# Fused GroupNorm attention block: normalisation of an image moved twelve slots ahead, and a new order of the first images' products

## The chip, the cores and the metric

One core of one Trainium2 chip runs the whole program in one launch. The metric is the device time of an execution in microseconds. The kernel before takes 1676.67 us (median of 3 runs, 1676.18 to 1676.68).

## The reference, cut to what matters

x has 16 images of 192 channels and 32 x 32 = 1024 positions, float32. Only a normalisation without weights, one attention block and the residual are computed:

```python
def _gn(v, G=32, eps=1e-05):
    g = v.reshape(B_, G, C_ // G, H_, W_)
    m = jnp.mean(g, axis=(2, 3, 4), keepdims=True)
    s = jnp.var(g, axis=(2, 3, 4), keepdims=True)
    return ((g - m) / jnp.sqrt(s + eps)).reshape(v.shape)
def attention(x, qkv_w, proj_w, proj_b):      # 6 heads of 32 channels, N = 1024
    xt = x.reshape(B, C, N).transpose(0, 2, 1)
    qkv = jnp.einsum('bnc,oc->bno', xt, qkv_w)
    q, k, v = ...
    attn = jax.nn.softmax(jnp.einsum('bhnd,bhmd->bhnm', q, k) * SCALE, axis=-1)
    out = jnp.einsum('bhnm,bhmd->bhnd', attn, v).transpose(0, 2, 1, 3).reshape(B, N, C)
    return (jnp.einsum('bnc,oc->bno', out, proj_w) + proj_b).transpose(0, 2, 1).reshape(B, C, H, W)
return x + attention(_gn(x), qkv_w, proj_w, proj_b)
```

## The kernel before, in words

**Steps and slots.** The program is a list of 20 steps, at = -3 to 16, and step b >= 0 attends to image b. A step has 24 slots: 3 pairs of heads, each with 8 tiles of 128 keys. A slot has 4 score units (two heads, two halves of 512 queries); "(5, 3)" is unit 3 of slot 5. Each engine has its own loop over steps, slots and units, and runs its instructions strictly in that order; nothing reorders them, and semaphores alone tie the engines together. Which slot a piece of work stands in is written out by hand in the tables at lines 57 to 80.

**What one slot does while a step attends.** TensorE makes 4 score products into 2 banks (line 535), ScalarE takes the exponential of each (line 690), TensorE weighs the values of the slot before (line 550, after unit 1), GpSimd adds the exponentials of two slots in pairs (line 743, in odd slots) and twice more in slots 3, 11 and 19 (line 749), and TensorE counts these sums (line 567). Beside that it makes 4 products for the row maxima of tiles 12 slots ahead, into 3 banks (line 469), and VectorE reduces each (line 844). From slot 12 of a step on these maxima are those of the next image, so in step -1 slots 12 to 23 make the maxima that image 0 needs before its first score. Scores of 2 banks mean that TensorE is at most two scores ahead of ScalarE, and maxima of 3 banks that it is at most three ahead of VectorE.

**Extras.** One PSUM bank, extra_ps, serves all other TensorE work, one extra in a slot (fill, line 473, in units 2 and 3), and the next extra waits until the one before is read (extra_freed). An extra is a "shift" (the transposed row maxima), a "v" product (read by ScalarE, line 613), a "qk" product (rounded by ScalarE, line 610, its remainder by VectorE, line 880), or a "proj" product (line 873). VectorE and ScalarE read an extra at the start of the slot after it. In step b, slots 3, 4 and 6 make qk products of image b+1, slots 7, 8, 11 and 14 its v, and slots 12, 16 and 19 the first qk products of image b+2. SyncE then stacks q and k with 18 DMAs in three sixes (slots 7, 9, 11, line 350). Step -2 makes all six qk products of image 0 (QK_FIRST_SLOTS) and stacks them, step -1 the v of image 0 and the first three qk products of image 1.

**The normalisation of image b+3 before.** x is loaded in slot 10 of step b (line 436, 3 DMAs), its statistics are taken by VectorE in slots 16 and 17 (line 776, 4 instructions), SyncE takes them to DRAM in slot 18 and back by groups in slot 20 (lines 370 and 375), VectorE aggregates in (22, 2) (line 786 to 790) and GpSimd makes the factors in slot 23 (lines 758 and 761). In step b+1 SyncE takes the factors to DRAM in slot 0 and back by channels in slot 1 (lines 358, 363, 365), ScalarE writes the normalised image in 8 instructions in slots 3 to 9 (line 642), and GpSimd the remainders in slots 8 and 10 (lines 708 and 718).

**SyncE.** It issues every DMA of the kernel in program order and waits in place for what a DMA needs. Around the change stand: the row shifts of a pair in slots 6, 14 and 22 (line 394, waited for by the first score of slots 8, 16 and 0), the sums spread in slots 5, 13 and 21 (line 400, waited for by VectorE's reciprocal at the end of slots 6, 14 and 22), their way back in slots 7/8, 15/16 and 23/0 (lines 407 and 413), the attention output's moves in slots 6, 14 and 23 (line 427), the residual's load in slot 4 (line 432) and the store of the image before in slot 23 (line 439).

Of the kernel before, what the change touches and what calls it, by code (L numbers as in the profile page):

```python
# [10 lines left out]
ALU = mybir.AluOpType  # L11
# [4 lines left out]
BATCH = 16  # L16
C = 192
# [4 lines left out]
GROUPS = 32  # L22
GROUP = C // GROUPS
# [4 lines left out]
P = 128  # L28
# [5 lines left out]
CB = C - P  # L34
# [22 lines left out]
SHIFT_SLOTS = {5: 1, 13: 2, 21: 0}  # L57


STATS_AT = ((16, 1), (16, 3), (17, 1), (17, 3))  # L60
STATS_OUT_SLOT, STATS_IN_SLOT = 18, 20
AGGREGATE_AT = (22, 2)
RSTD_SLOT = 23
NORM_OUT_SLOT, NORM_IN_SLOT = 0, 1
XHAT_AT = ((3, 3), (4, 1), (5, 3), (6, 1), (6, 3), (7, 3), (9, 1), (9, 3))
XLO_SLOTS = (8, 10)

QK_FIRST_SLOTS = (12, 13, 14, 15, 16, 17)
QK_SECOND_SLOTS = (17, 19, 22)
V_SECOND_SLOTS = (14, 15, 18, 20)  # L70
V_SLOTS = (7, 8, 11, 14)
QK_SLOTS = (12, 16, 19)
QK_LATE_SLOTS = (3, 4, 6)
# [3 lines left out]
assert len(set(EXTRA_SLOTS)) == len(EXTRA_SLOTS)  # L77
STACK_SLOTS = {7: 0, 9: 1, 11: 2}
QK_READERS = ((0, 1), (0, 2), (1, 2))
LOAD_SLOT = 10  # L80

PAIR = 2
PAIR_COUNTED = PAIR + 3
# [22 lines left out]
XHAT = 8  # L106
# [6 lines left out]
class Step:  # L113
# [5 lines left out]
    def __init__(self, b, at, extras):  # L119
        self.b = b  # L120
        self.parity = at % 2
        self.attend = 0 <= at < BATCH
        self.follow = 0 <= at + 1 < BATCH
        self.project_in = 0 <= at + 2 < BATCH
        self.take_stats = 0 <= at + 3 < BATCH
        self.tail = 0 <= at - 1 < BATCH
        self.qk_slots = {-2: QK_FIRST_SLOTS, -1: QK_SECOND_SLOTS}.get(at, QK_SLOTS)
        self.v_slots = V_SECOND_SLOTS if at == -1 else V_SLOTS
        self.late = at >= 0 and self.follow
        self.extras = extras  # L130

    def extra(self, s):

        if s in SHIFT_SLOTS and (self.follow if SHIFT_SLOTS[s] == 0 else self.attend):
            return "shift", SHIFT_SLOTS[s]
        if self.follow and s in self.v_slots:
            return "v", self.v_slots.index(s)
        if self.project_in and s in self.qk_slots:
            return "qk", self.qk_slots.index(s)
        if self.late and s in QK_LATE_SLOTS:  # L140
# [55 lines left out]
def group_norm_attention(nc, x, qkv_wT, proj_wT, proj_b, identity, out):  # L196


    with ExitStack() as ctx:
# [125 lines left out]
        def _(sp):  # L325
# [27 lines left out]
            def step(st):  # L353
                b = st.b
                for s in range(SLOTS):
                    if st.project_in and s == NORM_OUT_SLOT:
                        sp.wait_ge(rstd_step, 2 * (b + 3))
                        sp.dma_start(norm_rows[:, :].rearrange("(g c) k -> g c k", c=GROUP),
                                     group_norm[:, :].unsqueeze(1).broadcast_to([GROUPS, GROUP, 2])
                                     ).then_inc(norm_out, MOVE)  # L360
                    if st.project_in and s == NORM_IN_SLOT:
                        sp.wait_ge(norm_out, MOVE * (b + 3))
                        sp.dma_start(chan_norm[:, 0, :], norm_rows[0:P, :]).then_inc(norm_in, MOVE)
                        for r in range(2):
                            sp.dma_start(chan_norm[CB * r:CB * (r + 1), 1, :],
                                         norm_rows[P:C, :]).then_inc(norm_in, MOVE)
# [6 lines left out]
                    if st.take_stats and s == STATS_IN_SLOT:  # L373
                        sp.wait_ge(stats_out, 2 * MOVE * (b + 4))
                        sp.dma_start(group_stats[:, :],
                                     stats_rows[:, :].rearrange("(g c) k -> g (c k)", c=GROUP)
                                     ).then_inc(stats_in, MOVE)
                    if s == QK_FIRST_SLOTS[-1] + 1 and not st.follow and st.project_in:
# [50 lines left out]
                    if s == 4 and st.tail:  # L429
# [4 lines left out]
                    if s == LOAD_SLOT and st.project_in and b + 3 < BATCH:  # L434
                        sp.wait_ge(xhat_ready, XHAT * (b + 3))
                        load_x(b + 3)
# [160 lines left out]
        def _(act):  # L597
# [34 lines left out]
            def normalise(st, k):  # L632

                t, hi, half = k // 4, k // 2 % 2, k % 2
                if k == 0:
                    act.wait_ge(norm_in, 3 * MOVE * (st.b + 3))
                    if due(st.b + 2):

                        act.wait_ge(xlo_ready, LO * (st.b + 2))
                n = slice(HALF * half, HALF * (half + 1))  # L640
                to = (xhat[:, t, n], (xhat_a_hi, xhat_b)[t][:, st.parity, n])[hi]
                nc.scalar.activation(to, x_sb[:, t, n], ACT.Identity, bias=chan_norm[:, t, 1:2],  # L642
                                     scale=chan_norm[:, t, 0:1]).then_inc(xhat_ready, 1)

# [56 lines left out]
        def _(pool):  # L701
            nc.gpsimd.memset(k_stack[STACK:SHIFTED, :, :, :], SHIFT).then_inc(shift_set, 1)

            def step(st):
                for s in range(SLOTS):
                    if st.project_in and s == XLO_SLOTS[0]:
                        pool.wait_ge(xhat_ready, XHAT * (st.b + 2) + XHAT // 2)
                        nc.gpsimd.tensor_tensor(xhat_a_lo[:, st.parity, :], xhat[:, 0, :],  # L708
                                                xhat_a_hi[:, st.parity, :], ALU.subtract).then_inc(xlo_ready, 1)
                    if st.project_in and s == XLO_SLOTS[1]:  # L710
                        pool.wait_ge(xhat_ready, XHAT * (st.b + 3))

                        if st.attend:
                            was, q = divmod(s // PAIR - 1, PAIRS_A_HEAD)
                            pool.wait_ge(pairs_added, READY[-1] * (PAIRS * st.b + was) + READY[q])
                        else:
                            pool.wait_ge(xlo_ready, 2 * (st.b + 2) + 1)
                        nc.gpsimd.tensor_tensor(xhat_b[CB:P, st.parity, :], xhat[CB:P, 1, :],  # L718
                                                xhat_b[CB:P, st.parity, :], ALU.subtract).then_inc(xlo_ready, 1)
                        pool.wait_ge(xlo_ready, 2 * (st.b + 3))  # L720
                    for j, par, p in st.due(s, DIVIDED, TILES):

                        k = PAIRS * j + p
# [216 lines left out]
```

## Time and profile before

| what | number |
| --- | --- |
| median of 3 runs | 1676.67 us |
| the profiled execution | 1676.28 us |
| its span | 1674.5 us |
| mean granted TensorE clock | 0.982 |
| TensorE busy | 1556.8 us (93%) |
| VectorE, ScalarE, GpSimd busy | 1188.9, 1232.9, 1321.8 us |
| chain that ended last | TensorE 80%, ScalarE 10% |

The span runs from the first to the last instruction. Busy shares are averages over a start of some 112 us without scores, 16 steps of some 96 us, and an end of some 45 us. A matmul's end is modelled, so TensorE's busy time also covers short waits; its real waits are read from the starts of its instructions and from the waits of its weight loads.

### The profile page before, as it was taken

What the parts mean: (1) busy time and instruction counts of PE and PEld (TensorE: products, weight loads), DVE (VectorE), ACT (ScalarE), POOL (GpSimd) and SP (SyncE); (2) the same over time, 40 slices, a digit from 0 to 9 for tenths busy, and PEclk for the clock granted to TensorE, in tenths of its full rate; (3) what the DMA queues carried; (4) which work ended last, traced back from release to release, by engine and by line L of the source; (5) the groups of instructions that cost most, each with busy time, mean ns of one, the idle gap of its engine ahead of it and who ended that gap; (6) DMA issues with size and microseconds to landing.
All of it is one profiled execution on the core that took longest, in us unless ns stands there. A gap on an engine that the chain in (4) does not pass through costs nothing.

```text
span 1674.5 us, 24581 instructions
## 1 busy us (share of the span) xinstructions
PE 1556.8 (93%) x8800; PEld 488.0 (29%) x8800; DVE 1188.9 (71%) x2022; ACT 1232.9 (74%) x2001; POOL 1321.8 (79%) x645
## 2 busy tenths in 40 slices
PE   3389999999999999999999999999999999999982
PEld 1123233232323333232332323232332323233220
DVE  3387878777787877777787777778787777777710
ACT  2138787887869787886968788796978778686770
POOL 3019888888978888888888888897888888788891
PEclk9979999999999999999999999999999999999995
DMA  2304042341515134152504325151513414141112
GB/s 71 57 26 83 15 88 47 75 86 52 103 38 103 27 85 76 52 108 52 95 25 94 57 68 93 52 103 38 98 34 77 83 52 83 52 71 33 46 34 68
DMA packets 86106, 108.87 MB, mean 65 GB/s; under 512 B 38240, under 2 KB 50912, under 8 KB 85984
## 3 DMA queue, kind: packets, MB, share of 16 engines
q1 hardware_dynamic: 85984, 107.30, 30.8%
q8 instruction: 70, 1.15, 0.3%
q14 instruction: 52, 0.43, 0.1%
HBM read 42.98 MB, written 13.15 MB: 34 GB/s over the span
## 4 chain that ended last, share of the span: by engine, by line
PE 80%; ACT 10%; issue 2%; DMA 1%; DVE 1%; SPq 0%; POOL 0%; POOLq 0%; ACTq 0%; DVEq 0%
PE heads_ps L550 21%; PE scores_ps L535 19%; PE max_ps L469 19%; PE sums_ps L567 7%; ACT probs L690 6%; PE extra_ps L518 2%; PE extra_ps L522 2%; PE extra_ps L519 2%; PE extra_ps L520 2%; PE extra_ps L523 2%; ACT heads_sb L653 1%; ACT xhat_b L642 1%; ACT x_res L620 1%; DMA inv_sb<-inv_rows 1%; PE extra_ps L498 0%
## 5 line engine op out<-in xcount | busy, mean ns | idle before, releaser
L844 DVE TENSOR_REDUCE half_max<-max_ps 128x1 f32<-128x512 f32 x1536 | 1005.2, 685 | 336.0 <-PE max_ps L469 321.8
L690 ACT ACTIVATE probs<-scores_ps,exp_scale 128x512 f32<-128x512 f32 x1536 | 994.1, 689 | 310.4 <-PE scores_ps L535 304.5
L743 POOL TENSOR_TENSOR prob_pairs<-probs 128x1024 f32<-128x1024 f32 x384 | 898.6, 2361 | 205.1 <-ACT probs L690 204.2
L469 PE MATMUL max_ps<-k_stack,q_stack 96*128 96x512 f16 x1536 | 593.5, 388 | 22.5 <-DVE half_max L844 13.5
L535 PE MATMUL scores_ps<-q_stack,k_stack 98*128 98x512 f16 x1536 | 586.4, 383 | 24.4 <-ACT probs L690 18.2
L550 PE MATMUL heads_ps<-probs,v_sb 128*32 128x512 f32 x3072 | 409.8, 606 | 0.1
L469 PEld LDWEIGHTS max_ps<-k_stack,q_stack 96*128 96x128 f16 x1536 | 149.7, 98 | 555.5 <-issue 429.6
L749 POOL TENSOR_TENSOR prob_pairs<-prob_pairs 128x1024 f32<-128x1024 f32 x96 | 224.3, 2358 | 0.0
L535 PEld LDWEIGHTS scores_ps<-q_stack,k_stack 98*128 98x128 f16 x1536 | 149.5, 98 | 237.3 <-ACT probs L690 171.3
L567 PE MATMUL sums_ps<-prob_pairs,ones 128*32 128x512 f32 x1152 | 154.3, 608 | 3.2 <-POOL prob_pairs L743 3.2
L550 PEld LDWEIGHTS heads_ps<-probs,v_sb 128*32 128x32 f32 x3072 | 60.5, 108 | 131.7 <-issue 129.9
L880 DVE TENSOR_TENSOR qk_lo<-extra_ps,qk_hi 128x512 f16<-128x512 f32 x96 | 65.8, 686 | 33.4 <-ACT qk_hi L610 33.4
L727 POOL TENSOR_TENSOR heads_out<-heads_sb,inv_sb 128x512 f32<-128x512 f32 x48 | 61.0, 1271 | 32.8 <-DMA inv_sb<-inv_rows 26.8
L642 ACT ACTIVATE xhat<-x_sb,chan_norm 128x512 f32<-128x512 f32 x64 | 51.2, 806 | 46.3 <-DMA chan_norm<-norm_rows 46.3
L610 ACT CAST qk_hi<-extra_ps 128x512 f16<-128x512 f32 x96 | 56.0, 583 | 35.5 <-PE extra_ps L523 35.5
L873 DVE SCALAR_TENSOR_TENSOR x_res<-extra_ps,proj_unscale,x_res 96x512 f32<-96x512 f32 x64 | 46.1, 720 | 50.2 <-PE extra_ps L523 50.2
L758 POOL TENSOR_TENSOR group_norm<-var_eps,minus_half 32x1 f32<-32x1 f32 x16 | 8.6, 540 | 67.9 <-issue 64.2
L732 POOL TENSOR_TENSOR heads_lo<-heads_out,heads_hi 128x512 f16<-128x512 f32 x48 | 55.6, 1159 | 1.5 <-ACT heads_hi L630 1.5
L518 PE MATMUL extra_ps<-xhat_a_hi,w_hi 128*128 128x512 f16 x96 | 38.0, 396 | 17.9 <-POOL xhat_b L718 10.1
L708 POOL TENSOR_TENSOR xhat_a_lo<-xhat,xhat_a_hi 128x1024 f16<-128x1024 f32 x16 | 34.6, 2165 | 19.2 <-ACT xhat_a_hi L642 19.2
L776 DVE BATCH_NORM_STATS2 half_stats<-x_sb 128x6 f32<-128x512 f32 x64 | 43.3, 684 | 8.0 <-DMA x_sb<-x 8.0
L518 PE MATMUL extra_ps<-attn_a_hi,wp_hi 128*96 128x512 f16 x64 | 25.4, 397 | 22.9 <-DMA attn_b<-heads_lo 20.3
(82 smaller groups left out, 940.0 us busy)
## 6 DMA issues: line engine op xcount, KB each, us to landing
q_stack<-qk_hi SPq DMA_DIRECT2D x96, 128.0 KB, 4.2
k_stack<-qk_hi SPq DMA_DIRECT2D x96, 128.0 KB, 5.6
inv_sb<-inv_rows SPq DMA_DIRECT2D x48, 256.0 KB
x_res<-x SPq DMA_DIRECT2D x16, 768.0 KB, 5.5
out<-x_res SPq DMA_DIRECT2D x16, 768.0 KB, 4.6
x_sb<-x SPq DMA_DIRECT2D x16, 512.0 KB, 7.4
x_sb<-x SPq DMA_DIRECT2D x32, 256.0 KB, 8.7
q_stack<-qk_lo SPq DMA_DIRECT2D x48, 128.0 KB, 4.1
```

The costliest lines, as they stand in the source:

```text
L469: pe.matmul(max_ps[:, bank, :], q_stack[0:STACK, par, h, P * tile:P * (tile + 1)], k_stack[0:STACK, par, h, HALF * half:HALF * (half + 1)] ...
L518: pe.matmul(to, hi[:, 0, :], a_hi, start=True, stop=False)
L535: pe.matmul(scores_ps[:, u_bank(s, u), :], k_stack[0:SHIFTED, st.parity, h, P * tile:P * (tile + 1)], q_stack[0:SHIFTED, st.parity, h, HAL ...
L550: last = pe.matmul(heads_ps[at:at + D, :], v_sb[:, par, tile, D * h:D * (h + 1)], probs[:, a, s % RING, HALF * half:HALF * (half + 1)], st ...
L567: last = pe.matmul(sums_ps[at:at + D, :], ones[:, 0:D], prob_pairs[:, a, at_pair, HALF * half:HALF * (half + 1)], start=(at_pair == QUAD_A ...
L642: nc.scalar.activation(to, x_sb[:, t, n], ACT.Identity, bias=chan_norm[:, t, 1:2], scale=chan_norm[:, t, 0:1]).then_inc(xhat_ready, 1)
L690: nc.scalar.activation(probs[:, a, s % RING, HALF * half:HALF * (half + 1)], scores_ps[:, u_bank(s, u), :], ACT.Exp, scale=exp_scale[:, 0: ...
L727: nc.gpsimd.tensor_tensor(heads_out[:, :], heads_sb[:, (par + p) % 2, :], inv_sb[:, :], ALU.mult).then_inc(divided, 1)
L743: nc.gpsimd.tensor_tensor(prob_pairs[:, a, q, :], probs[:, a, (s - 1) % RING, :], probs[:, a, s % RING, :], ALU.add).then_inc(pairs_added, 1)
L749: nc.gpsimd.tensor_tensor(prob_pairs[:, a, q, :], prob_pairs[:, a, q, :], prob_pairs[:, a, q - 1, :], ALU.add).then_inc(pairs_added, 1)
L844: nc.vector.tensor_reduce(half_max[:, a, tile, half:half + 1], max_ps[:, bank, :], AX_X, ALU.max).then_inc(max_read[bank], 1)
L880: nc.vector.tensor_tensor(qk_lo[:, t, n], extra_ps[:, :], qk_hi[:, t, n], ALU.subtract).then_inc(extra_freed, 1)
```

## The change

The tables put the same work in other slots, and the blocks of SyncE, ScalarE and GpSimd are tied to the step that takes the statistics. The whole normalisation of image b+3 is now within step b: load in slot 0, statistics in slots 5 and 6, to DRAM in 7 and back in 9, aggregate in (10, 2), factors in 11, factors to DRAM in 12 and back in 13, the normalised image in unit 1 of slots 15 to 22, remainders in 19 and 23. In step -2 the six qk products of image 0 are in slots 0 to 5 and the 18 stacking DMAs in slot 6, ahead of the statistics' way out in slot 7. In step -1 the first qk products of image 1 are in slots 0, 2 and 4 and v of image 0 in slots 7, 8, 11 and 14. No instruction is added or removed.

```diff
-STATS_AT = ((16, 1), (16, 3), (17, 1), (17, 3))
-STATS_OUT_SLOT, STATS_IN_SLOT = 18, 20
-AGGREGATE_AT = (22, 2)
-RSTD_SLOT = 23
-NORM_OUT_SLOT, NORM_IN_SLOT = 0, 1
-XHAT_AT = ((3, 3), (4, 1), (5, 3), (6, 1), (6, 3), (7, 3), (9, 1), (9, 3))
-XLO_SLOTS = (8, 10)
-
-QK_FIRST_SLOTS = (12, 13, 14, 15, 16, 17)
-QK_SECOND_SLOTS = (17, 19, 22)
-V_SECOND_SLOTS = (14, 15, 18, 20)
+STATS_AT = ((5, 1), (5, 3), (6, 1), (6, 3))
+STATS_OUT_SLOT, STATS_IN_SLOT = 7, 9
+AGGREGATE_AT = (10, 2)
+RSTD_SLOT = 11
+NORM_OUT_SLOT, NORM_IN_SLOT = 12, 13
+XHAT_AT = ((15, 1), (16, 1), (17, 1), (18, 1), (19, 1), (20, 1), (21, 1), (22, 1))
+XLO_SLOTS = (19, 23)
+
+QK_FIRST_SLOTS = (0, 1, 2, 3, 4, 5)
+QK_SECOND_SLOTS = (0, 2, 4)
-LOAD_SLOT = 10
+LOAD_SLOT = 0
...
-        if self.follow and s in self.v_slots:
-            return "v", self.v_slots.index(s)
+        if self.follow and s in V_SLOTS:
+            return "v", V_SLOTS.index(s)
...
+                    if s == LOAD_SLOT and st.project_in and b + 3 < BATCH:
+                        sp.wait_ge(xhat_ready, XHAT * (b + 3))
+                        load_x(b + 3)
...
-                    if st.project_in and s == NORM_OUT_SLOT:
-                        sp.wait_ge(rstd_step, 2 * (b + 3))
+                    if st.take_stats and s == NORM_OUT_SLOT:
+                        sp.wait_ge(rstd_step, 2 * (b + 4))
...
-                    act.wait_ge(norm_in, 3 * MOVE * (st.b + 3))
-                    if due(st.b + 2):
+                    act.wait_ge(norm_in, 3 * MOVE * (st.b + 4))
+                    if due(st.b + 3):
...
-                to = (xhat[:, t, n], (xhat_a_hi, xhat_b)[t][:, st.parity, n])[hi]
+                to = (xhat[:, t, n], (xhat_a_hi, xhat_b)[t][:, 1 - st.parity, n])[hi]
...
-                if st.project_in and (s, u) in XHAT_AT:
+                if st.take_stats and (s, u) in XHAT_AT:
...
-                    if st.project_in and s == XLO_SLOTS[0]:
-                        pool.wait_ge(xhat_ready, XHAT * (st.b + 2) + XHAT // 2)
+                    if st.take_stats and s == XLO_SLOTS[0]:
+                        pool.wait_ge(xhat_ready, XHAT * (st.b + 3) + XHAT // 2)
```

## Rows read from the trace of the kernel before

**Rows 1.** Busy time by engine in step 6: us, PE, PEld, DVE, ACT, POOL, clock, DMA.

```profile
684.80:780.70 95.90, 94.73 (x551) 30.04 (x549) 73.64 (x126) 76.85 (x125) 81.88 (x41) 1.00 0.32 70
```

**Rows 2.** Timeline of the start: start us, us, instruction, [idle before, releaser].

```profile
10.22 0.85 SPq L370 DMA_DIRECT2D stats_rows<-half_stats  x2
...
14.02 0.47 DVE L786 BATCH_NORM_AGGREGATE group_mv<-group_stats 32x2 f32<-32x72 f32 x1 [1.23 <-DMA group_stats<-stats_rows]
...
22.26 1.52 ACT L642 ACTIVATE xhat<-x_sb,chan_norm 128x512 f32<-128x512 f32 x2 [20.24 <-DMA chan_norm<-norm_rows]
...
30.53 0.58 PE L518 MATMUL extra_ps<-xhat_a_hi,w_hi 128*128 128x512 f16 x1 [10.12 <-POOL xhat_b L718]
...
48.97 1.28 DVE L776 BATCH_NORM_STATS2 half_stats<-x_sb 128x6 f32<-128x512 f32 x2
...
52.80 0.64 SPq L350 DMA_DIRECT2D q_stack<-qk_hi  x1
...
64.41 0.58 SPq L375 DMA_DIRECT2D group_stats<-stats_rows  x1
69.92 0.47 DVE L786 BATCH_NORM_AGGREGATE group_mv<-group_stats 32x2 f32<-32x72 f32 x1 [17.15 <-DMA group_stats<-stats_rows]
...
71.59 0.61 SPq L358 DMA_DIRECT2D norm_rows<-group_norm  x1
...
78.08 1.52 ACT L642 ACTIVATE xhat<-x_sb,chan_norm 128x512 f32<-128x512 f32 x2 [26.04 <-DMA chan_norm<-norm_rows]
...
86.49 0.48 ACT L613 COPY v_sb<-extra_ps 128x384 f32<-128x384 f32 x1 [2.30 <-PE extra_ps L502]
...
112.58 0.63 PE L535 MATMUL scores_ps<-q_stack,k_stack 98*128 98x512 f16 x1
```

**Rows 3.** Timeline of VectorE in slots 5 to 7 of step 6.

```profile
706.09 2.47 DVE L844 TENSOR_REDUCE half_max<-max_ps 128x1 f32<-128x512 f32 x4
...
708.78 0.28 DVE L861 SCALAR_TENSOR_TENSOR shift_rows<-extra_ps,shift_rows 16x128 f16<-16x128 f32 x1
...
712.90 0.69 DVE L880 TENSOR_TENSOR qk_lo<-extra_ps,qk_hi 128x512 f16<-128x512 f32 x1 [0.40 <-ACT qk_hi L610]
```

**Rows 4.** Timeline of TensorE in slots 6 and 7 of step 6, the first matmul of each extra.

```profile
709.72 0.38 PE L518 MATMUL extra_ps<-xhat_a_hi,w_hi 128*128 128x512 f16 x1
...
713.74 0.25 PE L498 MATMUL extra_ps<-w_hi,xhat_a_hi 128*128 128x192 f16 x1
```

**Rows 5.** Waits, slots 4 to 10 of step 6: total us, times, longest.

```profile
PEld scores_ps L535 <- ACT probs L690: 2.8, 7, 0.9
```

**Rows 6.** Waits, slots 15 to 22 of step 6.

```profile
ACT probs L690 <- PE scores_ps L535: 9.6, 16, 1.4
...
PEld scores_ps L535 <- ACT probs L690: 1.5, 5, 0.5
```

**Rows 7.** Timeline of GpSimd in step 6: slot 0, slots 10 and 12.

```profile
686.82 0.54 POOL L758 TENSOR_TENSOR group_norm<-var_eps,minus_half 32x1 f32<-32x1 f32 x1
...
726.92 2.13 POOL L718 TENSOR_TENSOR xhat_b<-xhat,xhat_b 64x1024 f16<-64x1024 f32 x1
...
735.01 4.67 POOL L749 TENSOR_TENSOR prob_pairs<-prob_pairs 128x1024 f32<-128x1024 f32 x2
```

**Rows 8.** Timeline of SyncE in step 6: slots 0 and 14.

```profile
687.64 0.62 SPq L358 DMA_DIRECT2D norm_rows<-group_norm  x1
...
741.16 1.22 SPq L394 DMA_DIRECT2D q_stack<-shift_rows  x2
```

**Rows 9.** The 16 stores of the factors (line 358), from issue to landing.

```profile
DMA to landing us min/median/max: 3.3/4.1/5.6
```

**Rows 10.** Timeline of VectorE and ScalarE, end of slot 14 to slot 16 of step 6.

```profile
744.09 0.24 DVE L899 RECIPROCAL inv_spread<-sums_spread 128x16 f32<-128x16 f32 x1
...
745.67 1.27 ACT L690 ACTIVATE probs<-scores_ps,exp_scale 128x512 f32<-128x512 f32 x2 [0.60 <-PE scores_ps L535]
747.73 1.27 ACT L690 ACTIVATE probs<-scores_ps,exp_scale 128x512 f32<-128x512 f32 x2 [0.79 <-PE scores_ps L535]
```

More of the change, by code:

```diff
@@ L127, in __init__ @@
         self.qk_slots = {-2: QK_FIRST_SLOTS, -1: QK_SECOND_SLOTS}.get(at, QK_SLOTS)
-        self.v_slots = V_SECOND_SLOTS if at == -1 else V_SLOTS
         self.late = at >= 0 and self.follow
@@ L355, in step @@
                 for s in range(SLOTS):
-                    if st.project_in and s == NORM_OUT_SLOT:
-                        sp.wait_ge(rstd_step, 2 * (b + 3))
[L358 to L366, printed above, removed]
+                    if s == LOAD_SLOT and st.project_in and b + 3 < BATCH:
+                        sp.wait_ge(xhat_ready, XHAT * (b + 3))
+                        load_x(b + 3)
                     if st.take_stats and s == STATS_OUT_SLOT:
@@ L377, in step @@
                                      ).then_inc(stats_in, MOVE)
+                    if st.take_stats and s == NORM_OUT_SLOT:
+                        sp.wait_ge(rstd_step, 2 * (b + 4))
+                        sp.dma_start(norm_rows[:, :].rearrange("(g c) k -> g c k", c=GROUP),
+                                     group_norm[:, :].unsqueeze(1).broadcast_to([GROUPS, GROUP, 2])
+                                     ).then_inc(norm_out, MOVE)
+                    if st.take_stats and s == NORM_IN_SLOT:
+                        sp.wait_ge(norm_out, MOVE * (b + 4))
+                        sp.dma_start(chan_norm[:, 0, :], norm_rows[0:P, :]).then_inc(norm_in, MOVE)
+                        for r in range(2):
+                            sp.dma_start(chan_norm[CB * r:CB * (r + 1), 1, :],
+                                         norm_rows[P:C, :]).then_inc(norm_in, MOVE)
                     if s == QK_FIRST_SLOTS[-1] + 1 and not st.follow and st.project_in:
@@ L433, in step @@
                                      x[b - 1, :, :].rearrange("(t p) n -> p t n", p=OM)).then_inc(res_loaded, MOVE)
-                    if s == LOAD_SLOT and st.project_in and b + 3 < BATCH:
-                        sp.wait_ge(xhat_ready, XHAT * (b + 3))
-                        load_x(b + 3)
                     if s == SLOTS - 1 and st.tail:
@@ L635, in normalise @@
                 if k == 0:
-                    act.wait_ge(norm_in, 3 * MOVE * (st.b + 3))
-                    if due(st.b + 2):
-                        act.wait_ge(xlo_ready, LO * (st.b + 2))
+                    act.wait_ge(norm_in, 3 * MOVE * (st.b + 4))
+                    if due(st.b + 3):
+                        act.wait_ge(xlo_ready, LO * (st.b + 3))
                 n = slice(HALF * half, HALF * (half + 1))
-                to = (xhat[:, t, n], (xhat_a_hi, xhat_b)[t][:, st.parity, n])[hi]
+                to = (xhat[:, t, n], (xhat_a_hi, xhat_b)[t][:, 1 - st.parity, n])[hi]
                 nc.scalar.activation(to, x_sb[:, t, n], ACT.Identity, bias=chan_norm[:, t, 1:2],
@@ L705, in step @@
                 for s in range(SLOTS):
-                    if st.project_in and s == XLO_SLOTS[0]:
-                        pool.wait_ge(xhat_ready, XHAT * (st.b + 2) + XHAT // 2)
[L708 to L711, printed above, removed]
+                    if st.take_stats and s == XLO_SLOTS[0]:
+                        pool.wait_ge(xhat_ready, XHAT * (st.b + 3) + XHAT // 2)
+                        nc.gpsimd.tensor_tensor(xhat_a_lo[:, 1 - st.parity, :], xhat[:, 0, :],
+                                                xhat_a_hi[:, 1 - st.parity, :], ALU.subtract).then_inc(xlo_ready, 1)
+                    if st.take_stats and s == XLO_SLOTS[1]:
+                        pool.wait_ge(xhat_ready, XHAT * (st.b + 4))
                         if st.attend:
@@ L716, in step @@
                         else:
[L717 to L720, printed above, removed]
+                            pool.wait_ge(xlo_ready, 2 * (st.b + 3) + 1)
+                        nc.gpsimd.tensor_tensor(xhat_b[CB:P, 1 - st.parity, :], xhat[CB:P, 1, :],
+                                                xhat_b[CB:P, 1 - st.parity, :], ALU.subtract).then_inc(xlo_ready, 1)
+                        pool.wait_ge(xlo_ready, 2 * (st.b + 4))
                     for j, par, p in st.due(s, DIVIDED, TILES):
```

## The prediction

> **What bounds the kernel now.** I read the busy time of one steady step first, then the timeline of the start, then, slot by slot, the timelines around the old and the new places of the moved work. A steady step lasts 95.9 us and TensorE is busy in 94.7 of them [rows 1]; the other engines have 14 to 22 us to spare. So a moved piece costs something only where it makes TensorE wait, and helps only where TensorE waits for it now. The direct sign of such waits is the weight load of a score that waits for an exponential: 2.8 us in slots 4 to 10 of a step [rows 5] and 1.5 us in slots 15 to 22 [rows 6]. It starts earlier than the matmul's own wait, so it is an upper bound. Ahead of the steady steps stands a start of 112.6 us until the first score [rows 2], in which one image's chain of DMAs, statistics and products has nothing beside it.
>
> The sum is made against the profiled execution, 1676.28 us (span 1674.5), 0.4 us below the median of the runs. A measurement of this kernel tells some 0.2% (3.4 us) from no change.
>
> **1. The start: +21.6 us.** Up to the last first-image product nothing moves: first product at 30.5, q and k are stacked from 52.8 [rows 2]. What changes is what must come before the first row maximum. Before, TensorE makes maxima of image 0 while image 1 is still being normalised. After, its program has the qk products of image 1 (slots 0, 2, 4 of step -1) and three v extras ahead of slot 12, and VectorE has the statistics and the aggregate of image 2 ahead of it. All of that becomes serial:
> - The statistics of image 1 go out behind the 18 stacking DMAs, which take SyncE from 52.8 to 64.4. A transfer issued at 64.4 took 5.5 us until VectorE used it (69.9), where out and back together took 3.8 us when queues were empty (10.22 to 14.02). So out by 69.9, back 1.6 later: aggregate at 71.5, which was at 69.9. Bounds: 68.2 (3.8 for both) and 75.4 (5.5 for each).
> - Aggregate to the store of the factors 1.7 (69.92 to 71.59), to the first normalising instruction 6.5 (71.59 to 78.08), from there to the first qk product 8.3 (22.26 to 30.53): 88.0.
> - Three qk products at 3.7 each (six from 30.5 to 52.8): 99.1. Three v extras at 2.4 each (the row shows 2.30 + 0.48 with a maximum product of 0.4 in it): 106.3. Beside these, four statistics (1.28 for two [rows 2], the last two after the products), 3.8 for out and back and 0.7 for the aggregate end at about 106. Both give 106.
> - From there the first score needs 45 reductions at 0.6 (four in 2.47 [rows 3]) = 27.0 and 0.9 for a row shift and a negated maximum: 134.2, against 112.6 before. The difference is 21.6; the bounds of the first item and 2 us on the extras make it 18 to 26.
>
> **2. VectorE's statistics in slots 5 and 6: +1.05 us a step.** VectorE has no room there: from 706.09 it runs four reductions and the row shift without a gap [rows 3]. Two statistics of 0.6 ahead of the shift move its end from 709.06 to 710.3. The qk extra of slot 6 waits for that to free the bank and starts at 709.72 now [rows 4]: TensorE waits 0.65. Two more statistics and the reciprocal move the read of that product from 712.90 to 714.2, its end to 714.85; the v extra of slot 7, at 713.74 now [rows 4] and 714.4 after the first wait, waits 0.45 more. Together 1.1, of which 0.05 was a wait for ScalarE anyway. Bounds 0.3 (if the maxima are reordered by the banks more kindly than I see) and 1.3. What the statistics leave, slots 16 and 17, holds no wait of TensorE for VectorE and gives nothing. The aggregate (0.7) goes from (22, 2) to (10, 2), a slot without an extra: hidden behind TensorE's three banks, at most 0.2 without it.
>
> **3. ScalarE's eight normalisations leave slots 3 to 9: -0.4 us a step.** They take 8 x 0.8. At best the whole 2.8 [rows 5] goes; at worst nothing, since the bias additions of slots 10 and 11 and the copies stay. In slots 15 to 22, with no normalisation in them, the same wait is 1.5 [rows 6], so the share of the normalisation is at most 1.3; a weight load's wait is two or three times the matmul's here, so 0.4. It counts in 14 steps (0 to 13).
>
> **4. They arrive in slots 15 to 22: +0.1 us a step.** ScalarE waits 9.6 us for scores there [rows 6] and 6.5 come in, one to a slot. Only slots 20 and 21 are tight (a rounding, two copies and two normalisations), and slots 4 and 5 hold the same set now. Bounds 0 and 0.5.
>
> **5. The factors' way in slots 11 to 15: +0.6 us a step.** This is the new wait. GpSimd makes the factors in slot 11 behind two pair sums and two more sums, which end at 739.68 [rows 7]. The remainder that stood ahead of them (726.92, 2.13 long) is gone, which may bring their end forward by 1.1 at most: 738.6. From the start of the factors to SyncE's store 0.8 (686.82 to 687.64 [rows 7, 8]): issued at 739.4. From such a store to the first normalisation the quiet start took 6.5 [rows 2], with a landing of 3.3, the least of the 16 [rows 9]: 745.9; with the median 4.1 it is 746.7. Three things stand behind:
> - ScalarE reaches unit 1 of slot 15 at about 745.0, waits 0.9 to 1.7 and works 0.7; the exponentials due at 745.67 come at 746.6 to 747.4. It had 0.79 to spare before slot 16 [rows 10], so TensorE loses 0.1 to 0.9.
> - SyncE waits for the landing at slot 13, and its three loads (1.5), the spread of the sums (0.6) and then the row shifts of pair 2 queue behind: from 741.16 [rows 8] to about 744.9 or 745.7, two issues and 1.8 of landing, 747.9 to 748.7, where the first score of slot 16 ran at 747.2 (its exponential at 747.73 [rows 10]): 0.7 to 1.5 less what the first item already delays.
> - VectorE's reciprocal at 744.09 [rows 10] waits for the spread sums until about 746.3; TensorE's three banks cover 2 of that.
> They lie beside each other, so the largest counts: 0.1 to 1.5, and 2.6 if GpSimd is not 1.1 earlier. I take 0.6, near the quiet landing, because the DMA burst of slots 7 to 11 is over by then and the load of x no longer stands in it. The attention moves and the way back of the inverted sums follow 4 us later; the proj extra of slot 17 has 5 us for them: nothing.
>
> A landing of 3.3 to 5.6 us [rows 9] is what makes this wait. The Trainium skill, DMA: Bandwidth & Descriptors, section Anatomy of one DMA — SWDGE (gpsimd) path, gives a fixed cost of about 2.0 us for a transfer (of that path; these go by SyncE). By it the factors would be back before ScalarE asks, part 5 would be zero and the sum 7.8 us less, an estimate from that page; the trace does not agree with it for this store.
>
> **6. The rest: 0.** x is loaded right behind the store of slot 23 and ahead of the inverted sums of slot 0, which GpSimd needs in slot 3: 1.8 of issues and a queue, against 2.1 us that it idles around there; I expect its product some 1 to 3 us later and no wait of TensorE. Slots 10 and 11 lose three DMAs: the last stacks land earlier, nobody waits for them. GpSimd's remainders go to slots 19 and 23, in front of probabilities that come later; in slot 19 they use a gap of 3 us. Without that cover each costs up to 2.1 of GpSimd and reaches ScalarE through its ring of four slots.
>
> **Sum.** Steps 0 to 12 have parts 2, 4 and 5: 13 x (1.05 + 0.1 + 0.6) = 22.8. Part 3: 14 x -0.4 = -5.6. Start 21.6. 1676.3 + 21.6 + 22.8 - 5.6 = 1715.
>
> **The rivals.**
> - **The steady steps break even**: the bank order absorbs part 2 and the factors are back in time. Then 1676.3 + 21.6 - 4 = 1694. For it: TensorE is two scores and three maxima ahead. Against: VectorE has no gap in slot 5. Chance 0.22.
> - **The factors come late in full**: landing 4.5, GpSimd not earlier, part 5 at 2.4 a step: 1676.3 + 21.6 + 13 x 3.55 - 5.6 = 1738. Chance 0.18.
> - **Faster**: ScalarE's relief in slots 3 to 10 is worth more than the start. It decides from 21.6 / 14 = 1.55 us a step. With the whole 2.8 of [rows 5], parts 2 and 5 absorbed: 1676.3 + 21.6 - 39.2 = 1659. Against it: the same wait is 1.5 where nothing is normalised. Chance 0.05.
> - **No change within 0.2%**: the relief just pays for the start. Chance 0.03.
> - That the change does not do what it says is excluded by its form: the tables are run literally, in order.
>
> **Numbers.** The forecast has 0.52. The range, 1692 to 1738, goes from the break-even case to the late factors and so holds the bounds of parts 1, 2 and 5. Faster 0.05, same 0.03, slower 0.92.
>
> **What the profile after would show.** Part 1: the first score near 134, row maxima from 106, none before. Part 2: the qk extra of slot 6 waiting for VectorE. Part 5: in slot 15 the first normalisation with idle time before it, released by chan_norm, and the stores' landings near 3.5. Steps of about 97.3 us. It would be wrong if the first score came before 125, or if steps were not longer than 95.9.

## The result, and the profile after

The changed kernel takes 1748.19 us (median of 4 runs, 1743.83 to 1750.31) where the kernel before takes 1676.43 us: ratio 1.0426, 95% interval 1.0405 to 1.0446. It is slower by 72 us, where 39 were forecast, and lies outside the range of 1692 to 1738. The profiled execution took 1750.31 us with a span of 1748.5, against 1676.28 and 1674.5 before. The changed kernel has the same instructions under other line numbers, since its file is two lines shorter and SyncE's store of the factors stands elsewhere in it: line 844 before is 842 after, 690 is 688, 358 is 370.

The page of the changed kernel, its chain by engine and by line:

```profile
PE 52%; DMA 11%; ACT 9%; SPq 8%; DVE 5%; issue 5%; POOL 3%; POOLq 0%; ACTq 0%; DVEq 0%
PE heads_ps L548 13%; PE scores_ps L533 13%; PE max_ps L467 12%; ACT probs L688 6%; PE sums_ps L565 6%; DMA group_stats<-stats_rows 5%; SPq L348 3%; DVE half_max L842 3%; DMA inv_rows<-inv_spread 2%; SPq L428 2%; DMA norm_rows<-group_norm 2%; PE extra_ps L516 2%; PE extra_ps L517 1%; PE extra_ps L518 1%; POOL prob_pairs L741 1%
```

TensorE held 80% of the chain before; it holds 52% now, and the largest new entry is a DMA of 9 KB, the statistics' way back from DRAM (group_stats<-stats_rows, 5%). That is not the wait that the prediction put first. Step 6 by windows, the row that answers to [rows 1]:

```profile
728.50:828.20 99.70, 95.37 (x551) 29.82 (x549) 73.42 (x126) 77.02 (x125) 81.90 (x41) 1.00 0.31 68
```

**Where the time went**, by the starts of the 1536 exponentials (a slot lasts from its first exponential to that of the next; means over steps 2 to 12, us):

| | before | after | forecast of the difference | measured |
| --- | --- | --- | --- | --- |
| first exponential | 113.2 | 135.4 | +21.6 | +22.2 |
| slots 5 to 7 | 11.50 | 12.59 | +1.05 | +1.09 |
| slots 8 to 10 | 11.15 | 11.15 | -0.4 (with 3 to 7) | 0 |
| slot 11 | 4.91 | 7.02 | 0 | +2.11 |
| slots 15 and 16 | 7.96 | 8.88 | +0.6 | +0.92 |
| slots 18 to 22 | 20.12 | 20.18 | +0.1 | +0.06 |
| step | 95.94 | 100.12 | +1.35 | +4.2 |

From the first exponential to that of step 13 it is 1294.7 us after 1243.1 (+51.6), and with the 22.2 of the start that is 73.8 of the 74.0 us of span. Slot 11 alone holds 2.11 x 12 = 25 us: what the forecast lacked.

**Slot 11.** Timelines of the changed kernel in step 6, one of the milder steps (slot 11 lasts 5.89 us in it, 7.02 on average): SyncE around slot 9, VectorE at the end of slot 10, TensorE in slot 11.

```profile
765.97 0.59 SPq L414 DMA_DIRECT2D inv_sb<-inv_rows  x1
766.61 0.47 SPq L365 DMA_DIRECT2D group_stats<-stats_rows  x1
...
773.82 0.47 DVE L784 BATCH_NORM_AGGREGATE group_mv<-group_stats 32x2 f32<-32x72 f32 x1 [2.07 <-DMA group_stats<-stats_rows]
...
774.46 1.86 DVE L842 TENSOR_REDUCE half_max<-max_ps 128x1 f32<-128x512 f32 x3
...
775.18 0.39 PE L467 MATMUL max_ps<-k_stack,q_stack 96*128 96x512 f16 x1 [0.91 <-DVE half_max L842]
```

The way back is issued at 766.61, right behind the 256 KB broadcast of the inverted sums (765.97), and VectorE can aggregate only at 773.82. It stands 2.07 us there with the row maxima behind it, and TensorE, whose three banks are full, stops until 775.18. Before, the same transfer was issued with nothing beside it (median landing of its 16 issues 1.5 us); of the 16 issues after:

```profile
DMA to landing us min/median/max: 1.5/7.4/8.2
```

Six stacking DMAs of 128 KB each stand ahead of the way back and twelve right behind it, so it has more company than the broadcast. Step 0 of the same kernel tells them apart: it has these stacks on both sides and no broadcast in slot 8, since that one belongs to the last pair of the image before. The landing of its way back, issued at 167.09:

```profile
DMA to landing us min/median/max: 3.6/3.6/3.6
```

That is 3.6 us with the stacks alone and 6.8 or more in every later step, with the broadcast ahead, and slot 11 of step 0 lasts 4.91 us as before. Of the 7.4 us, 1.5 is what the transfer took alone, some 2 come with the stacks and some 4 with the broadcast.

TensorE's clock has a part in slot 11 too. In steps 5 and 10 that slot lasts 8.91 and 10.26 us, in the other ten steps 5.7 to 7.1, and in those two alone the granted clock fell at the stop. Three microseconds of each by windows: the stretch, its length, busy time of PE, PEld, DVE, ACT and POOL, the clock as a share of its upper level, DMA share and GB/s:

```profile
675.50:678.50 3.00, 3.00 (x13) 1.82 (x14) 2.40 (x4) 0.99 (x2) 1.70 (x1) 0.50 0.95 141
1177.50:1180.50 3.00, 2.66 (x11) 1.51 (x12) 2.44 (x5) 0.69 (x1) 2.06 (x1) 0.50 1.01 151
```

0.50 is the lower of the two levels, 1.2 GHz in place of 2.4. The other steps follow the aggregate alone (it starts 46.50 us into step 2 and slot 11 is 7.11; it starts 46.73 and 46.80 us into steps 5 and 10), so I estimate the clock's share at 1.6 + 2.8 = 4.4 of the 25 us.

**Slot 15.** The chain of waits of the changed kernel, slots 13 to 15 of step 6 (slot 15 lasts 5.51 us in it, 4.81 on average): start, us, what.

```profile
782.09 2.36 POOL prob_pairs L747
784.44 0.50 POOL group_norm L756
...
785.23 3.23 DMA norm_rows<-group_norm
...
788.84 0.50 SPq L377
789.35 0.04 issue
789.39 2.10 SPq L377
791.49 0.04 issue
791.53 1.86 DMA sums_spread<-sums_sb
793.39 0.02 issue
793.41 0.25 DVE inv_spread L897
793.66 0.56 DVE half_max L842
```

This is part 5 of the prediction as written: factors behind GpSimd's sums, the landing on SyncE, the spread of the sums queued behind it, VectorE's reciprocal, the maxima. ScalarE waits there too (from 790.9 to 792.93). The store's landing was 3.4 us (median of 16; 4.1 in [rows 9]), as near the quiet one as assumed. What was not foreseen is the start of the chain, GpSimd: the store of the factors goes out 57.6 us into a step on average, forecast 739.4 less 684.8, 54.6. The last load of the factors, whose issue took 2.10 us here, is a chance of this step: such an issue took over 2 us in 3 of 32 cases in this kernel and in 2 of 32 in the kernel before, and 0.6 in the median.

```profile
773.34 1.28 POOL L725 TENSOR_TENSOR heads_out<-heads_sb,inv_sb 128x512 f32<-128x512 f32 x1 [1.73 <-DMA inv_sb<-inv_rows]
...
779.77 4.67 POOL L747 TENSOR_TENSOR prob_pairs<-prob_pairs 128x1024 f32<-128x1024 f32 x2
784.40 0.54 POOL L756 TENSOR_TENSOR group_norm<-var_eps,minus_half 32x1 f32<-32x1 f32 x1
```

In that timeline of GpSimd the division waits for the broadcast (all 48 divisions wait 88.6 us after, 26.8 before), so the missing remainder of slot 10 brings nothing forward.

**The start.** Timeline of the changed kernel, lines that answer to [rows 2]:

```profile
63.80 1.10 SPq L360 DMA_DIRECT2D stats_rows<-half_stats  x2
69.31 0.32 SPq L365 DMA_DIRECT2D group_stats<-stats_rows  x1
70.93 0.47 DVE L784 BATCH_NORM_AGGREGATE group_mv<-group_stats 32x2 f32<-32x72 f32 x1 [17.57 <-DMA group_stats<-stats_rows]
...
87.40 0.59 PE L516 MATMUL extra_ps<-xhat_a_hi,w_hi 128*128 128x512 f16 x1 [36.58 <-POOL xhat_b L716]
...
98.39 2.46 DVE L774 BATCH_NORM_STATS2 half_stats<-x_sb 128x6 f32<-128x512 f32 x4
...
105.48 6.90 DVE L842 TENSOR_REDUCE half_max<-max_ps 128x1 f32<-128x512 f32 x11 [0.19 <-PE max_ps L467]
...
134.70 0.63 PE L533 MATMUL scores_ps<-q_stack,k_stack 98*128 98x512 f16 x1
```

Aggregate 70.9 (forecast 71.5), first product of image 1 87.4 (88.0), maxima from 105.5 (106), first score 134.7 (134.2).

### The profile page after: what moved, and what is told of

It is laid out like the page before. It is cut to its first block, busy times and chain, and to the rows that moved or that the text cites. A ratio compares the mean times of both kernels' runs of the same rounds, so it can differ in the third digit from the quotient of the medians.

```text
span 1748.5 us, 24582 instructions
## 1 busy us (share of the span) xinstructions
PE 1574.9 (90%) x8800; PEld 487.5 (28%) x8800; DVE 1185.7 (68%) x2022; ACT 1236.0 (71%) x2001; POOL 1321.1 (76%) x645
## 4 chain that ended last, share of the span: by engine, by line
PE 52%; DMA 11%; ACT 9%; SPq 8%; DVE 5%; issue 5%; POOL 3%; POOLq 0%; ACTq 0%; DVEq 0%
PE heads_ps L548 13%; PE scores_ps L533 13%; PE max_ps L467 12%; ACT probs L688 6%; PE sums_ps L565 6%; DMA group_stats<-stats_rows 5%; SPq L348 3%; DVE half_max L842 3%; DMA inv_rows<-inv_spread 2%; SPq L428 2%; DMA norm_rows<-group_norm 2%; PE extra_ps L516 2%; PE extra_ps L517 1%; PE extra_ps L518 1%; POOL prob_pairs L741 1%
## 5 line engine op out<-in xcount | busy, mean ns | idle before, releaser
L725 POOL TENSOR_TENSOR heads_out<-heads_sb,inv_sb 128x512 f32<-128x512 f32 x48 | 61.0, 1271 | 88.6 <-DMA inv_sb<-inv_rows 88.6
L516 PE MATMUL extra_ps<-attn_a_hi,wp_hi 128*96 128x512 f16 x64 | 25.4, 397 | 24.2 <-DMA attn_b<-heads_lo 21.6
```

The costliest lines, as they stand in the source:

```text
L516: pe.matmul(to, hi[:, 0, :], a_hi, start=True, stop=False)
L725: nc.gpsimd.tensor_tensor(heads_out[:, :], heads_sb[:, (par + p) % 2, :], inv_sb[:, :], ALU.mult).then_inc(divided, 1)
```

## The experiments

Each time is a median of the runs beside the kernel before on the same chip, which gave 1675.1 to 1675.6 us. The slot lengths are means over steps 2 to 12 of the profiled execution, as above.

**1. The statistics' way back ahead of the broadcast.**

```diff
-STATS_OUT_SLOT, STATS_IN_SLOT = 7, 9
+STATS_OUT_SLOT, STATS_IN_SLOT = 7, 8
```

> The changed kernel with the statistics' way back in slot 8, ahead of the broadcast of the inverted sums and of the second stacking, in place of slot 9. My theory: in steps 1 to 12 slot 11 lasts 7.0 us instead of 4.9 because VectorE stands at the aggregate of (10, 2) until these statistics land, 7 us after their issue, behind the broadcast; with this edit slot 11 is 4.9 again. It also says that the two new waits cover one another: step 0 of the changed kernel, where slot 11 is not longer, has slot 15 at 6.2 (3.9 before), so slot 15 grows from 4.8 to about 6.2 in every step and the net gain is 0.7 us a step, 9 us in all: 1739 us. Rival: the waits are independent, slot 15 stays at 4.8 and 13 x 2.1 = 27 us go: 1721 us. Second rival: the aggregate's wait comes from somewhere else and slot 11 stays at 7.0: 1748 us.

Measured: 1757.5 us, ratio 1.0481 (1.0453 to 1.0509). The landing fell to a median of 2.7 us, VectorE's waits at the aggregate from 55.8 us in 15 to 22.7 in 3 (the start's), and slot 11 was 4.91 us: the cause of slot 11 is shown. But the kernel did not gain. Slots 15 and 16 took 11.7 us where they were 8.9, 3.8 more than in the kernel before. Of these 3.8, slot 15 has 2.8 (6.75 us after 3.93): that is the cost of part 5 with nothing in front of it. GpSimd and VectorE in step 6 of this kernel:

```profile
778.43 1.26 POOL L725 TENSOR_TENSOR heads_out<-heads_sb,inv_sb 128x512 f32<-128x512 f32 x1 [3.15 <-DMA inv_sb<-inv_rows]
...
788.91 0.54 POOL L756 TENSOR_TENSOR group_norm<-var_eps,minus_half 32x1 f32<-32x1 f32 x1
...
797.56 0.25 DVE L897 RECIPROCAL inv_spread<-sums_spread 128x16 f32<-128x16 f32 x1 [4.89 <-DMA sums_spread<-sums_sb]
```

GpSimd waits 3.15 us for the broadcast, makes the factors 10.5 us later, and VectorE stands 4.89 us before the reciprocal. In the changed kernel the stop in slot 11 delays TensorE and ScalarE while this chain goes on, and so hides most of it: the spread of the sums is issued 63.1 us into a step in both kernels (means over steps 2 to 12), and only slot 15 starts earlier here, at 60.1 in place of 62.2.

Covering alone can't make a kernel slower. Added up over steps 0 to 12 of the two profiled executions, slot 11 gives back 24.9 us, slot 15 takes 23.4, and slot 16 takes another 11.5, though nothing was moved into it. Slot 16 of steps 5 and 6 of this kernel by windows:

```profile
697.40:703.20 5.80, 5.80 (x23) 1.67 (x22) 3.20 (x6) 4.21 (x8) 2.36 (x1) 0.71 0.24 68
799.20:803.30 4.10, 4.10 (x23) 1.37 (x22) 3.30 (x6) 4.05 (x7) 2.33 (x1) 1.00 0.23 52
```

TensorE runs 23 matmuls in both, with a mean clock of 0.71 in the first, 0.50 in the three microseconds from 698:

```profile
698.00:701.00 3.00, 3.00 (x12) 0.58 (x5) 1.48 (x3) 1.85 (x4) 1.81 (x1) 0.50 0.20 46
```

Over all fourteen traces slot 16 of steps 0 to 12 lasts more than 5 us (5.2 to 6.6) in 21 cases, and these are the cases in which the granted clock fell to 1.2 GHz around its start; in all others it lasts 3.9 to 4.1. Six of the 21 are in this kernel, none in the changed kernel or the one before. TensorE had stood still for 1.6 to 4.6 us in slot 15 each time, but there are steps with 2.9 us and no fall. No run keeps the clock up through such a stop, so its part rests on this agreement. So the loss of 9 us is the covered wait, nearly in full, and the lower clock behind it. My theory had the covering right, its size too small and no clock in it (a gain of 9 us forecast, a loss of 9 found); the rival of independent waits fell.

**2. Without the statistics in slots 5 and 6.**

```diff
+                if b >= 0:
+                    dve.sem_inc(stats_step, 1)
+                    return
                 nc.vector.bn_stats(half_stats[:, t, half, :],
```

> The changed kernel without VectorE's four statistics instructions in steps 0 to 12 (their semaphore counts are kept, so images 3 to 15 are normalised with the statistics of image 2). Theory: the four instructions of 0.6 us in slots 5 and 6 make TensorE wait for the freed bank in slots 6 and 7; slots 5 to 7 go from 12.6 us back to 11.5 (11.4 where ScalarE also has no normalisation there), 1.1 to 1.2 us a step, about 14 us: 1734 us. Rival: they are hidden by the three banks and slots 5 to 7 are longer because SyncE and the shift are late for another reason; then slots 5 to 7 stay at 12.6 and the time at 1748 us.

Measured: 1737.8 us, ratio 1.0377 (1.0352 to 1.0403). Slots 5 to 7 were 11.41 us, 1.18 less than with the statistics. So part 2 is shown and its size with it. The time fell by 10 us and not by 13 x 1.18 = 15, since slot 11 rose to 7.34 on average; in five steps the clock fell to 1.2 GHz there. The 0.09 us by which 11.41 is below the 11.50 of the kernel before is all that ScalarE's relief gives there.

**3. The factors' way after the shifts.**

```diff
-NORM_OUT_SLOT, NORM_IN_SLOT = 12, 13
-XHAT_AT = ((15, 1), (16, 1), (17, 1), (18, 1), (19, 1), (20, 1), (21, 1), (22, 1))
-XLO_SLOTS = (19, 23)
+NORM_OUT_SLOT, NORM_IN_SLOT = 14, 16
+XHAT_AT = ((17, 3), (18, 1), (18, 3), (19, 1), (20, 1), (21, 1), (21, 3), (22, 1))
+XLO_SLOTS = (20, 23)
```

> The changed kernel with the factors' store in slot 14 in place of 12, their loads in slot 16 in place of 13 and the eight normalisations from (17, 3) to (22, 1), the first remainder in slot 20. So the spread of the sums and the row shifts of pair 2 no longer stand behind the wait for the store's landing. Theory: slot 15 goes from 4.8 to 3.9 us and nothing else moves: 13 x 0.9 = 12 us less, 1736 us, with slot 11 still at 7.0 us. Rival: the wait only moves to slot 17, where ScalarE asks for the factors now, and the time stays at 1745 to 1748 us.

Measured: 1737.9 us, ratio 1.0381 (1.0356 to 1.0406). Slot 15 was 3.93 us in every step, slot 11 stayed at 6.76, slots 18 to 22 at 20.18 in all. The wait did not move to slot 17 (4.93 us, as in the kernel before).

**4. Both edits.** Experiments 1 and 3 in one kernel.

> Both edits in one, way back of the statistics in slot 8 and the factors' way in slots 14 and 16. Theory: what covered the one wait was the other, so together they give more than the sum of the two alone: slots 11 and 15 go back to 4.9 and 3.9 us, the steady step from 100.0 to 97.0 us, 39 us less in all: 1709 us, of which 22 us are the longer start and 14 us VectorE's statistics in slots 5 and 6. Rival (independent waits): the same 1709 us, but then the first edit alone gives 27 us. Rival (late load in slot 17): 1715 to 1725 us.

Measured: 1714.4 us, ratio 1.0230 (1.0214 to 1.0245). Slots 11 and 15 were 4.91 and 4.04, the step 97.2 us. On the same chip the first edit alone gave 1757.5 and the second 1737.9: with the factors late, the statistics' way back is worth 23.5 us; the difference of 43.1 us between experiment 1 and this one is the factors' way with slot 11 free, some 12 of it the lower clock of slot 16. What is left over the kernel before, 15.3 us in thirteen steps (nearly all of it in slots 5 to 7) and 23.0 of start, is 38 us of the 39 measured.

**5. Both edits and no statistics.**

> The kernel with the statistics back in slot 8 and the factors in slots 14 and 16, and in it no statistics instructions of VectorE in steps 0 to 12 (semaphore counts kept; images 3 to 15 use the statistics of image 2). Theory: with that the last of the three waits is gone and a steady step is 95.9 us again (97.1 with the statistics), so 1714.4 - 12 to 15 = 1701 us, and what is left over 1676 is the start alone (23 us). Rival: the statistics hide behind another wait here and the time stays above 1710 us.

Measured: 1698.5 us, ratio 1.0138 (1.0124 to 1.0151). Its step 6 by windows, beside 95.90 in [rows 1]:

```profile
706.90:802.80 95.90, 94.66 (x551) 30.03 (x549) 71.58 (x122) 76.63 (x126) 81.64 (x41) 1.00 0.34 70
```

The three waits are all there is in the steady steps. With them gone a step is as long as before (95.95 us on average, 95.94 before): moving ScalarE's eight normalisations, here to slots 17 to 22, neither costs nor gains anything. What remains, 23 us, is nearly all the start (21.7 us in the profiled execution).

**6. The products of image 1 after the maxima again.**

```diff
-QK_SECOND_SLOTS = (0, 2, 4)
+QK_SECOND_SLOTS = (17, 19, 22)
```

> The changed kernel with the first three qk products of image 1 in slots 17, 19 and 22 of step -1 again, in place of 0, 2 and 4; all else as changed. My theory of the start: image 0's row maxima stand behind image 1's qk products, three v extras and image 2's statistics. Taking the products out lets the statistics of image 2 be taken some 9 us earlier, since x of image 2 comes at about 93; the maxima then start near 98 in place of 106, but the three products (0.7 us of VectorE each and the wait for their bank) stand among them. First exponential at about 129 in place of 135.4, so some 6 us less: 1742 us, with the steady steps as they are. Rival: the start hangs on the load and statistics of image 2 alone: first exponential at 135, 1748 us. Second rival: it hangs on the products alone: near 124, 1737 us.

Measured: 1745.2 us, ratio 1.0422 (1.0405 to 1.0439). The first exponential came at 132.2, 3 us earlier in place of 6, and step 0 was 97.3 us in place of 94.5. The gain of the time is inside the scatter of this kernel. It does not tell the theories apart well: the products are a small part of what stands ahead of the maxima.

**7 and 8. The kernel before, with its own start mended.** Experiment 7 has the first edit, experiment 8 both.

```diff
-STATS_OUT_SLOT, STATS_IN_SLOT = 18, 20
+STATS_OUT_SLOT, STATS_IN_SLOT = 18, 18
```

> The kernel before, with the statistics' way back in slot 18 in place of 20, so that in step -2 it is issued ahead of the 18 stacking DMAs of image 0 and not behind them. In the kernel before this transfer was issued at 64.4 and used at 69.9, and VectorE stood at the aggregate until then with image 0's row maxima (the first filled at 60) behind it. Theory: the aggregate is done by about 55, the maxima run from 60, but image 1's normalisation is freed only from 71.6 to about 65, since the store of its factors still stands behind the stacks on SyncE, and the v extras wait for that: first score near 106 in place of 112.6: 1670 us. Rival: VectorE is not what the start waits for and the time stays at 1676 us. Steady steps stay at 95.9.

Measured: 1671.4 us, ratio 0.9977 (0.9968 to 0.9986). The first exponential came at 111.2 in place of 113.2; a gain, but of 4 us and not 6.

```diff
-                        for p in range(PAIRS):
-                            stack_pair(st.parity, p)
+                        stack_pair(st.parity, 0)
+                    if s in (2, 3) and b == -1:
+                        stack_pair(1 - st.parity, s - 1)
```

> As the one before it, and of the 18 stacking DMAs of image 0 only the six of pair 0 stay in slot 18 of step -2; pairs 1 and 2 follow in slots 2 and 3 of step -1, behind the factors' way out and in. Theory: the store of image 1's factors is issued at about 57 in place of 71.6 and its normalisation ends near 70 in place of 83.9, so the first score comes near 99: 1663 us. Rival: row maxima of image 0, 45 reductions from 60 on and what stands among them, bind by themselves, and it is no faster than the one before it, 1670 us. Steady steps stay at 95.9.

Measured: 1663.7 us, ratio 0.9929 (0.9916 to 0.9941), the fastest kernel of this study, 11 us less than the kernel before and 8 less than experiment 7. Timeline of its start:

```profile
51.40 0.32 SPq L375 DMA_DIRECT2D group_stats<-stats_rows  x1
...
53.06 0.47 DVE L787 BATCH_NORM_AGGREGATE group_mv<-group_stats 32x2 f32<-32x72 f32 x1 [1.22 <-DMA group_stats<-stats_rows]
...
55.77 0.61 SPq L358 DMA_DIRECT2D norm_rows<-group_norm  x1
...
63.65 1.52 ACT L643 ACTIVATE xhat<-x_sb,chan_norm 128x512 f32<-128x512 f32 x2 [12.53 <-DMA chan_norm<-norm_rows]
...
101.17 0.38 PE L536 MATMUL scores_ps<-q_stack,k_stack 98*128 98x512 f16 x1
```

Normalisation of image 1 starts at 63.65 where it was 78.08 [rows 2], and the first score is at 101.2 where it was 112.6. The rival, that the maxima bind by themselves, falls.

**9. Stacking of pair 1 in slot 10.**

```diff
-STACK_SLOTS = {7: 0, 9: 1, 11: 2}
+STACK_SLOTS = {7: 0, 10: 1, 11: 2}
```

> The changed kernel with the stacking of pair 1 in slot 10 in place of 9, so that its six DMAs are issued after the wait of slot 9 and not right behind the statistics' way back; the order of SyncE's DMAs is otherwise the same, so the six come a little later or not at all later, since SyncE does not wait between slots 9 and 10. Theory: what delays the landing of the statistics (7.4 us median) is the broadcast of the inverted sums issued ahead of them, not what follows; nothing changes: slot 11 near 7.0 us, 1745 to 1750 us. This is the control for the first experiment, where the statistics went ahead of the broadcast and landed in 2.7 us. Rival: the number of the slot matters by itself; slot 11 gets shorter.

Measured: 1762.9 us, ratio 1.0529 (1.0511 to 1.0546). The edit turned out to change nothing: every engine has the same instructions in the same order as in the changed kernel, so it is no control but a repetition. Slot 11 was 7.07 us and the landing's median 7.5, as expected; slots 15 and 16 were 9.5 us. The same program took 15 us more than in its first measurement, with the kernel before at 1675.5 beside it. Of the 10.7 us by which the two profiled executions differ, 6.5 stand in slot 16, where the clock fell in four steps, 3.2 in slot 15, 0.9 in slot 11 and 0.7 in the start.

**10. The factors made ahead of the sums.** Experiment 1, and in it:

```diff
-RSTD_SLOT = 11
+RSTD_SLOT = 10
```

> The changed kernel with the statistics' way back in slot 8 (as in the first experiment, 1757 us) and the factors made by GpSimd in slot 10 in place of 11, so ahead of the division, the two pair sums and the two further sums of slot 11. Theory: in the first experiment slot 15 takes 6.8 us because GpSimd starts the division only when the broadcast lands (46.2 us into the step) and the factors stand behind 10.5 us of its work; made in slot 10 they leave SyncE in slot 12 right away and are back before ScalarE asks in slot 15. So slot 15 is 3.9 us, slot 11 is 4.9 us, the steady step 97.1 us and the time 1714 us, as in the kernel whose consumers came later. Rival: SyncE's wait for the landing itself is what holds the spread of the sums and the row shifts, whenever the factors are made; slot 15 stays above 5 us and the time above 1730 us.

Measured: 1716.4 us, ratio 1.0244 (1.0228 to 1.0259). Slot 15 was 3.95 us and the step 97.1. One slot earlier on GpSimd takes 41 us off experiment 1, the lower clock of slot 16 included: no step shows it here. SyncE in step 6 of this kernel:

```profile
762.82 0.62 SPq L370 DMA_DIRECT2D norm_rows<-group_norm  x1
770.32 0.32 SPq L375 DMA_DIRECT2D chan_norm<-norm_rows  x1
```

It still waits 7.5 us here for the landing, since the store goes behind the last stacks, but nobody is late for it. So SyncE's wait is harmful only with its start behind GpSimd's sums.

**11 and 12. The changed kernel and experiment 1 again, on one chip.**

> The changed kernel as it is, on one chip with the next. The run before last turned out to have the same order of instructions on every engine as the changed kernel, and took 1762.9 us where that had taken 1748.2. Theory: the new waits in slots 11 and 15 hang on the landing of DMAs, which differs between executions and chips, so the changed kernel has no one time: anything from 1744 to 1766 us, beside the kernel before at 1674 to 1678 us. Rival: it is 1748 us within 0.3% everywhere and the other run was disturbed.

> The first experiment again (statistics back in slot 8), on the same chip as the changed kernel. Theory: slot 11 is 4.9 us, slots 15 and 16 take the 2 us over, and the difference to the changed kernel on the same chip is small, between 12 us less and 9 us more. Rival (independent waits): 25 us less than the changed kernel on this chip.

Measured: 1747.9 us (1744.4 to 1751.7; ratio 1.0433, 1.0412 to 1.0454) and 1757.2 us (ratio 1.0484, 1.0469 to 1.0499). On one chip experiment 1 is 9 us slower than the changed kernel, so its loss is real. The changed kernel gave 1748, 1748 and 1763 us in three sessions. The trace of the third shows longer stops and the clock falling behind them; why they are longer there was not tried.

## Why the prediction was wrong, point by point

- **Part 1, the start (+21.6): right.** Measured +22.2, and each station of the chain within 0.6 us.
- **Part 2, statistics in slots 5 and 6 (+1.05): right in place and size**, 1.18 by experiment 2. The two reads ended where they were put: the bank of slot 6 free at 754.1 less 728.5 is 25.6 us into the step, forecast 710.3 less 684.8, 25.5. The product of slot 7 starts at 758.58, 30.1 into the step, forecast 714.85 less 684.8, 30.05.
- **The end of part 2 failed**: "The aggregate (0.7) goes from (22, 2) to (10, 2), a slot without an extra: hidden behind TensorE's three banks, at most 0.2 without it." This is the step that made the forecast wrong. I priced the aggregate by VectorE's 0.7 us of work and did not ask when its data lands. Part 6 looks at SyncE's queue in slots 0, 10 and 11 only; nowhere did I put the way back of slot 9 behind the broadcast of slot 8. The runs show 7.4 us of landing in place of 1.5, and 2.1 us a step, 25 of the 33 us by which the forecast missed.
- **Part 3, ScalarE's relief (-0.4): wrong in size**, 0.1 in all by experiment 2 against the kernel before, in slots 5 to 7; slots 8 to 10 are the same to 0.01 us. The weight loads' wait for exponentials in slots 4 to 10 of step 6 did fall, from 2.8 [rows 5] to 2.0 us, and the slots did not: that wait was hardly TensorE's. I took a weight load's wait as two or three times the matmul's; the traces have 171.3 us against 18.2 over the whole kernel before, and 2.8 against 0.4 in these slots.
- **Part 4 (+0.1): right**, 0.06.
- **Part 5, the factors (+0.6, bounds 0.1 to 2.6): right mechanism, wrong size.** Measured 0.9 in the changed kernel, which looks right, but that is luck: slot 11 covers the rest. Alone it is 2.8 in slot 15 (experiment 1), a little above my upper bound, and 0.9 more in slot 16 by the lower clock, a term that no part of the prediction has. The step that failed here is that GpSimd would be 1.1 us earlier without the remainder: the division was waiting for the broadcast. The Trainium skill, DMA: Bandwidth & Descriptors, section Anatomy of one DMA — SWDGE (gpsimd) path, gives a fixed cost of about 2.0 us for a transfer of another path. By it, as an estimate, this part would have been zero; the runs do not agree, since such a store landed in 3.1 to 4.8 us in the changed kernel.
- **Part 6 (0): right on the load of x.** GpSimd waits 3.7 us for the broadcast in slots 0 to 4 of step 6, where it waited 0.8 before, and these five slots last 20.54 us in both kernels.
- **The rivals.** The late-factor rival (1738) named what is the largest wait once slot 11 is free, but the time above it came from the aggregate, which no rival had. The break-even rival and the faster one fell with experiments 2 and 5.

## What to carry to other kernels

When a small DMA is moved, list what stands ahead of it in the queue at its new place, and take the landing from a transfer in such company, not from the one it had before. In a schedule written out by hand a wait must be priced from the moment its data is made, through every in-order queue in between, and two waits in a row can hide one another: taking the first away (experiment 1) only handed its time to the second, taking both gave 34 us. When a kernel gets slower where the covering allows no more than a tie, read the granted clock behind the longer stop. And a start that is serial deserves its own look: the two edits of experiment 8 were worth 0.7%, the 12 later DMAs alone 0.5%.

## What the runs showed of the hardware that was not expected

A 9 KB transfer issued 0.6 us behind a 256 KB broadcast out of DRAM landed after 7.4 us (median of 16), after 3.6 us with the same stacks around it and no broadcast (step 0), and after 2.7 us when it was issued ahead of the broadcast. A stop of TensorE can cost more than its length: when the granted clock fell from 2.4 to 1.2 GHz behind a stop, the next slot lasted 5.7 us in most cases in place of 4.1, and the same matmul 0.63 us in place of 0.38. That was 11.5 us in experiment 1. What decides whether it falls was not tried. The time of the program with these waits differed by up to 15 us between sessions (1748 to 1763), while the kernel before stayed within 1675.1 to 1676.4: once DMA landings are on the path, their scatter is in the time, and the clock can multiply it.
